# Splitting the input's first normalization into one batch a pass on GpSimd, and the bulk loads into pieces, in a four-layer attention kernel

## The reference

```
h = layernorm(x)                      # "LN0": no weight or bias, eps 1e-5
for l in range(4):
    xn = LN(h) * ln1_w + ln1_b
    q, k, v = xn@Wq.T+bq, xn@Wk.T+bk, xn@Wv.T+bv     # 16 heads of 8
    scores = (q.k + relshift((q+u).r)) / sqrt(8), causal
    h = h + softmax(scores) @ v @ Wo.T + bo
    h = h + gelu(LN(h) @ W1.T + b1) @ W2.T + b2      # inner size 512
x = x + h
x = x + moe(layernorm(x))             # 16 experts, top 4 in 2 of 4 groups, plus a shared one
```

## Time and profile before

| | |
|---|---|
| median of 3 runs | 2402.88 us |
| the profiled execution's own time | 2404.88 us |
| its span in the trace | 2403.1 us |
| PE busy | 2285.8 us (95%) |
| DVE busy | 2023.2 us (84%) |
| ACT busy | 1837.5 us (76%) |
| POOL busy | 1146.4 us (48%) |
| mean busy share of the DMA engines | 3 to 5 tenths until the expert part |

### The profile page before, as it was taken

The page is one execution under the profiler, slowest core; times in us unless marked ns, Lnnn a source line. Parts: engine busy times, 40 slices in busy tenths (PEclk is TensorE's granted clock), DMA queues, the critical chain, the costliest instruction groups (busy, mean ns, idle before and its releaser), DMA issues. The chain is left out here.

```text
span 2403.1 us, 83241 instructions
## 1 busy us (share of the span) xinstructions
PE 2285.8 (95%) x31360; PEld 1976.7 (82%) x31360; DVE 2023.2 (84%) x5071; ACT 1837.5 (76%) x2869; POOL 1146.4 (48%) x2089
## 2 busy tenths in 40 slices
PE   3899999999999999999999999999999999799998
PEld 3688888888888888888888888888888888677776
DVE  6789999888888888888888888888888886677774
ACT  2578888888888888888888888888878888655554
POOL 4355555554555555555454555555445553333332
PEclk8799999999999999999999999999999999899999
DMA  5543333333333333333333333333333331000000
GB/s 130 117 105 97 88 86 91 91 86 92 88 86 91 95 91 92 92 92 85 92 91 93 86 89 91 91 92 91 88 102 88 90 92 51 21 27 27 27 23 19
DMA packets 221161, 196.05 MB, mean 82 GB/s; under 512 B 28897, under 2 KB 217441, under 8 KB 220769
## 3 DMA queue, kind: packets, MB, share of 16 engines
q1 hardware_dynamic: 220768, 190.73, 29.8%
HBM read 14.46 MB, written 4.19 MB: 8 GB/s over the span
## 5 line engine op out<-in xcount | busy, mean ns | idle before, releaser
L1012 DVE TENSOR_REDUCE rowmax<-bank 128x4 f32<-128x1024 f32 (+1 forms) x768 | 914.2, 1218 | 103.3 <-PE bank L580 74.9
L817 ACT ACTIVATE probs<-bank 128x1024 f32<-128x1024 f32 x768 | 738.2, 1024 | 79.4 <-PE bank L640 78.8
L580 PE MATMUL bank<-kstack,qstack 62*128 62x256 f32 (+1 forms) x4096 | 417.9, 301 | 9.5 <-DMA qstack<-base 9.5
L640 PE MATMUL bank<-qstack,kstack 64*128 64x128 f32 (+1 forms) x4096 | 424.3, 300 | 0.0
L858 ACT ACT_TABLE_LOAD x256 | 328.4, 1283 | 4.5
L580 PEld LDWEIGHTS bank<-kstack,qstack 62*128 62x128 f32 x4096 | 317.4, 193 | 9.9 <-issue 9.9
L640 PEld LDWEIGHTS bank<-qstack,kstack 64*128 64x128 f32 x4096 | 317.1, 192 | 0.0
L602 PE MATMUL bank<-maskT_half,pick_half 64*128 64x128 bf16 (+1 forms) x3072 | 267.9, 241 | 24.5 <-DVE rowmax L1012 10.9
L542 PE MATMUL bank<-mask_half,pick_half 64*128 64x128 bf16 (+1 forms) x3072 | 268.8, 243 | 7.9 <-DVE h_all L1047 3.1
L725 PE MATMUL bank<-w,hidden 128*128 128x128 f32 x2048 | 272.6, 277 | 3.1 <-ACT hidden L867 3.1
L660 PE MATMUL bank<-probs,v_pad 128*32 128x256 f32 x4096 | 271.4, 382 | 0.6 <-DVE v_tok L993 0.6
(11 more groups left out here) (154 smaller groups left out, 5259.7 us busy)
## 6 DMA issues: line engine op xcount, KB each, us to landing
qstack<-base SPq DMA_DIRECT2D x768, 128.0 KB, 2.5
kstack<-base SPq DMA_DIRECT2D x384, 128.0 KB, 2.5
turn_x<-turn_c SPq DMA_DIRECT2D x512, 32.0 KB, 1.8
qstack<-maxrows SPq DMA_DIRECT2D x256, 16.0 KB
out<-ot SPq DMA_DIRECT2D x16, 256.0 KB, 2.4
xin<-in_x SPq DMA_DIRECT2D x14, 256.0 KB, 3.1
w<-in_w SPq DMA_DIRECT2D x4, 256.0 KB, 3.2
w_in<-in_w_in SPq DMA_DIRECT2D x1, 768.0 KB, 4.3
```

What stands on the lines that cost most here:

```text
L580: last = pe.matmul(bank[:, b0 + b, i * wide:(i + 1) * wide], qstack[rows, r, p0 + i, t * 128:(t + 1) * 128], kstack[rows, r, p0 + i, 0:wid ...
L640: last = pe.matmul(bank[:, b0 + b, i * wide:(i + 1) * wide], kstack[rows, r, p0 + i, kt * 128:(kt + 1) * 128], qstack[rows, r, p0 + i, q0: ...
L817: act.activation(probs[:, k], bank[:, A_BANK[k]:A_BANK[k] + 2, :], ACT.Exp, scale=SCALE).then_inc(exp_done[k], 1)
L1012: dve.tensor_reduce(rowmax[:, n % 2, t, :, p0:p0 + heads], bank[:, M_BANK[k]:M_BANK[k] + 2, :].rearrange("p b (h c) -> p b h c", h=heads), ...
```

## The change

LN0 groups become two of two batches (0 and 1, 2 and 3) and then 28 of one batch. From pass 1 to pass 28, each pass has `stats_0` of one batch (two tiles) on DVE, at the place where it stood, and `power_0` and a new `normalize_0` on POOL, at the place of `power_0`, ahead of the two `add_row`s. `apply_0` stays on DVE for groups 0 and 1 only; `stats_0(2)` and `power_0(2)` leave pass -1. The bulk loads are cut and spread: x in chunks of four batches (0.52 MB) in passes 1, 4, 7, 10, 13 and 16; b_o and w_o in pass 2; w_1 in pass 3; b_2 and b_1 in pass 4; w_2 by layer (0.26 MB) in passes 5, 7, 9 and 11; the q, k, v weights by layer (0.20 MB) in passes 12, 14 and 17. `split_w1(0)` moves on POOL from pass 3 to 4. Waits are divided accordingly (`middle_landed`, `later_landed`, `w_rest_landed`).

```diff
-PER = 2
-LN0_FIRST = 2
+LN0_STARTS = (0, 2) + tuple(range(4, 32))
+LN0_MOST = max(hi - lo for lo, hi in zip(LN0_STARTS, LN0_STARTS[1:] + (32,)))
-X_STARTS = (0, 2, 4, 8, 16, 24)
+X_STARTS = (0, 2, 4, 8, 12, 16, 20, 24, 28)
...
             def loads_behind(s):
-                if s == 1:
-                    rows_of_x(3)
                 if s == 2:
-                    sp.dma_start(b_o[:], on_all("bo")).then_inc(later_landed, 16)
+                    sp.dma_start(b_o[:], on_all("bo")).then_inc(middle_landed, 16)
+                    sp.dma_start(w_o[:], a["w_o"].rearrange("l p n -> p l n")).then_inc(middle_landed, 16)
+                if s == 3:
                     sp.dma_start(w_1[:], a["w_1"][0]).then_inc(w1_landed, 16)
-                    sp.dma_start(w_o[:], a["w_o"].rearrange("l p n -> p l n")).then_inc(later_landed, 16)
-                if s == 3:
+                if s == 4:
                     sp.dma_start(b_2[:], on_all("b2")).then_inc(later_landed, 16)
                     sp.dma_start(b_1[:], a["b_1"].rearrange("p (l c) -> p l c", l=LAYERS)).then_inc(later_landed, 16)
-                    sp.dma_start(w_2[:], a["w_2"].rearrange("l (c p) n -> p l c n", p=128)).then_inc(later_landed, 16)
-                if s in (4, 8):
-                    rows_of_x(3 + s // 4)
-                if s == 10:
-                    sp.dma_start(w_qkv[:, 1:LAYERS], a["w_qkv"].rearrange("l p n -> p l n")[:, 1:LAYERS]
-                                 ).then_inc(w_rest_landed, 16)
+                if s >= 5 and s % 2 == 1 and s // 2 - 2 < LAYERS:
+                    ly = s // 2 - 2
+                    sp.dma_start(w_2[:, ly], a["w_2"].rearrange("l (c p) n -> p l c n", p=128)[:, ly]
+                                 ).then_inc(later_landed if ly == 0 else w_rest_landed, 16)
+                if s >= 1 and s % 3 == 1 and 3 + s // 3 < len(X_STARTS):
+                    rows_of_x(3 + s // 3)
+                if s in (12, 14, 17):
+                    ly = 1 + (12, 14, 17).index(s)
+                    sp.dma_start(w_qkv[:, ly], a["w_qkv"][ly]).then_inc(w_rest_landed, 16)
...
             # DVE's pass
-                if s % PER == 0 and LN0_FIRST <= s // PER + 2 < B // PER:
-                    apply_0(s // PER + 2)
-                if s % PER == 1 and LN0_FIRST <= s // PER + 3 < B // PER:
-                    stats_0(s // PER + 3)
+                if 2 <= s + 1 < len(LN0_STARTS):
+                    stats_0(s + 1)
...
             # POOL
+            def normalize_0(g):
+                lo, hi = ln0_group(g)
+                pool.wait_ge(rstd0_ready, g + 1)
+                for i in range((hi - lo) * T):
+                    tile = h_all[:, lo + i // T, i % T]
+                    last = pool.tensor_scalar(tile, tile, mv0[:, i, 0:1], rstd0[:, i:i + 1], ALU.subtract, ALU.mult)
+                last.then_inc(ln0_done, 1)
...
-                if s > 0 and s % PER == 1 and LN0_FIRST <= s // PER + 3 < B // PER:
-                    power_0(s // PER + 3)
+                if 2 <= s + 1 < len(LN0_STARTS):
+                    power_0(s + 1)
+                    normalize_0(s + 1)
                 if live(s - 6):
-                    add_row(s - 6, b_2, xn2_ready, 2 * (s - 5), b2_added)
+                    add_row(s - 6, b_2, later_landed, LATER_DMAS, xn2_ready, 2 * (s - 5), b2_added)
                 if live(s - 4):
-                    add_row(s - 4, b_o, xn1_ready, 2 * (s - 3), bo_added)
+                    add_row(s - 4, b_o, middle_landed, MIDDLE_DMAS, xn1_ready, 2 * (s - 3), bo_added)
...
                 if s == -1:
                     power_0(1)
-                    power_0(2)
...
-                if s == 3:
+                if s == 4:
                     split_w1(0)
```

More of the change, by code:

```diff
@@ L99, in bank_left, with ln0_group @@
             return
+def ln0_group(g):
+    return (LN0_STARTS + (B,))[g:g + 2]
 def at_least(eng, sem, value):
@@ L239, in layers_program @@
         expo = sb("expo", [128, 16])
[L241 to L244, removed]
+        stats0 = sb("stats0", [128, LN0_MOST * T, 6])
+        mv0 = sb("mv0", [128, LN0_MOST * T, 2])
+        ve0 = sb("ve0", [128, LN0_MOST * T])
+        rstd0 = sb("rstd0", [128, LN0_MOST * T])
         stats1 = sb("stats1", [128, T, 6])
@@ L289, in layers_program @@
         consts_landed = sem("consts_landed")
+        middle_landed = sem("middle_landed")
         later_landed = sem("later_landed")
@@ L376, in layers_program @@
         CONST_DMAS = 4
-        LATER_DMAS = 5
+        MIDDLE_DMAS, LATER_DMAS, REST_DMAS = 2, 3, 2 * (LAYERS - 1)
         SLOTS = range(-LEAD, N + LAG)
@@ L691, in b3 @@
                 if n == 0:
-                    pe.wait_ge(later_landed, 16 * LATER_DMAS)
+                    pe.wait_ge(middle_landed, 16 * MIDDLE_DMAS)
                 bank_left(pe, (live(n + 3), max_done[4], n + 4), (live(n), ctxT_ready, n + 1))
@@ L722, in down @@
                     pe.wait_ge(gelu_done, FC * (n + 1))
+                    if n == 0:
+                        pe.wait_ge(later_landed, 16 * LATER_DMAS)
+                    if n == B:
+                        pe.wait_ge(w_rest_landed, 16 * REST_DMAS)
                     bank_left(pe, (live(n + 3), exp_done[5], n + 4), (live(n), gelu_done, FC * (n + 1)))
@@ L925, in stats_0 @@
             def stats_0(g):
-                dve.wait_ge(x_landed[sum(start <= g * PER for start in X_STARTS) - 1], 16)
+                lo, hi = ln0_group(g)
+                for c in range(len(X_STARTS)):
+                    if lo <= X_STARTS[c] < hi or X_STARTS[c] <= lo < (X_STARTS + (B,))[c + 1]:
+                        dve.wait_ge(x_landed[c], 16)
                 at_least(dve, rstd0_ready, g)
-                for i in range(PER * T):
-                    last = dve.bn_stats(stats0[:, i], h_all[:, g * PER + i // T, i % T])
+                for i in range((hi - lo) * T):
+                    last = dve.bn_stats(stats0[:, i], h_all[:, lo + i // T, i % T])
                 last.then_inc(stats0_done, 1)
                 dve.wait_ge(stats0_done, g + 1)
-                for i in range(PER * T):
+                for i in range((hi - lo) * T):
                     last = dve.bn_aggr(mv0[:, i], stats0[:, i])
@@ L936, in apply_0 @@
             def apply_0(g):
+                lo, hi = ln0_group(g)
                 dve.wait_ge(rstd0_ready, g + 1)
-                for i in range(PER * T):
-                    tile = h_all[:, g * PER + i // T, i % T]
+                for i in range((hi - lo) * T):
+                    tile = h_all[:, lo + i // T, i % T]
                     last = dve.tensor_scalar(tile, tile, mv0[:, i, 0:1], rstd0[:, i:i + 1], ALU.subtract, ALU.mult)
@@ L962, in stats_1 @@
             def stats_1(n):
-                dve.wait_ge(ln0_done, min(n, B - 1) // PER + 1)
+                dve.wait_ge(ln0_done, sum(start <= n for start in LN0_STARTS))
                 at_least(dve, h2_ready, n - B + 1)
@@ L1155, in power_0 @@
                 at_least(pool, ln0_done, g)
-                pool.tensor_scalar(ve0[:], mv0[:, :, 1], 1e-5, None, ALU.add).then_inc(ve0_ready, 1)
+                lo, hi = ln0_group(g)
+                c = (hi - lo) * T
+                pool.tensor_scalar(ve0[:, 0:c], mv0[:, 0:c, 1], 1e-5, None, ALU.add).then_inc(ve0_ready, 1)
                 pool.wait_ge(ve0_ready, g + 1)
-                pool.tensor_tensor(rstd0[:], ve0[:], expo[:, 0:PER * T], ALU.pow).then_inc(rstd0_ready, 1)
+                pool.tensor_tensor(rstd0[:, 0:c], ve0[:, 0:c], expo[:, 0:c], ALU.pow).then_inc(rstd0_ready, 1)
+            def normalize_0(g):
+                lo, hi = ln0_group(g)
+                pool.wait_ge(rstd0_ready, g + 1)
+                for i in range((hi - lo) * T):
+                    tile = h_all[:, lo + i // T, i % T]
+                    last = pool.tensor_scalar(tile, tile, mv0[:, i, 0:1], rstd0[:, i:i + 1], ALU.subtract, ALU.mult)
+                last.then_inc(ln0_done, 1)
             def power(ve, mv, rstd, mv_sem, ve_sem, rstd_sem, n):
@@ L1168, in split_qkv @@
                 at_least(pool, qk_done, B * (ly - 1))
-                if ly == 1:
-                    pool.wait_ge(w_rest_landed, 16)
+                if ly > 0:
+                    pool.wait_ge(w_rest_landed, 16 * REST_DMAS)
                 w, high = w_qkv[:, ly, 0:2 * D], w_now[:, ly % 2, 0]
@@ L1223, in v_padded, with add_row @@
                 last.then_inc(vpad_ready, 1)
-            def add_row(n, rows, read_sem, value, added_sem):
+            def add_row(n, rows, landed, dmas, read_sem, value, added_sem):
                 pool.wait_ge(read_sem, value)
                 if n == 0:
-                    pool.wait_ge(later_landed, 16 * LATER_DMAS)
+                    pool.wait_ge(landed, 16 * dmas)
                 h = h_all[:, n % B]
```

## The result

The changed kernel took 2444.07 us (median of 5, 2439.67 to 2446.11) against 2402.88 us before: a ratio of 1.0164, 95% interval 1.0151 to 1.0177, 41 us slower by the medians (39 by the ratio) where 7.8 us faster was forecast. Its profiled execution, 2439.67 us, is the fastest of the five, and that of before, 2404.88 us, is slower than its median, so the two spans differ by only 34.6 us.

A forecast was written before the change was run, and what follows sets the result against it. PE was taken to bound passes without LN0 or loads, DMA passes 0 to 5 and 8. Terms -9.0 (passes 0 to 5), -1.0 (steady loads) and +2.2 (LN0) gave -7.8: 2397.1 us profiled, 2395.1 median, range 2387 to 2402.

The forecast's parts named there:

- y: Time of two normalizations on POOL in each pass with LN0, taken as 0.62 us, 0.31 each.
- y - 0.02: Excess of each pass with LN0, 0.60 us in 23 passes: 13.8 us against 11.6 before, net +2.2.
- two of the large additions: Upper bound for POOL's two normalizations, 1.46 us, priced from two-input operations of 256 elements; it gives +21.5 us.
- a pass of LN0 over 16.3 us: Sign that the prediction is wrong, with POOL's two normalizations taking over 1 us.
- The slow rival: On POOL between power_0 and the add_rows: normalizations of 1.2 us set every pass, total 2408.4 us; chance 0.14.
- the rival in which the relief of DVE pays in full: DVE's load makes the LN0 passes' excess; a pass would cost 0.1 us, LN0 -9.3 us, total 2383.6; chance 0.08.
- the steady loads: Bulk loads in the steady passes after the fill: net -1.0 us, bounds -2.4 and +2.
- The fill: Passes 0 to 5, fewer bulk bytes ahead of the stacks: together -9.0 us, bounds -5 and -13.
- that term: Passes 4 and 5: fewer bytes in pass 4 shrink PE's wait for resid_1(0); -2.2 us, bounds 1.0 and 4.5.
- The rival of a fill that is paced by work: DVE and PE at low clock set passes 2 to 5; only -5.5 us comes back, total 2398.6; chance 0.18.
- a lone chunk of 0.52 MB: Chunks of x in passes 10, 13 and 16: set at no cost, with 0.3 us of margin as cover.
- part 1 and 2: Bulk bytes ahead of the stacks in passes 0 to 5, -9.0 us, and bulk in the steady passes, -1.0 us.

The follow-up runs named there:

- e3: The changed kernel with both add_rows on POOL moved ahead of power_0 and normalize_0; 2389.65 us, 0.9938 of the kernel before.
- e5: The changed kernel with POOL's order add_rows, normalize_0 of the group from the pass before, then power_0; 2387.14 us, 0.9926 of the kernel before.
- m1: A kernel of its own without the computation, timing POOL's elementwise forms and DVE's tensor_scalar beside POOL's additions; POOL's tensor_scalar with two SBUF scalars took 0.80 us.
- e6: The changed kernel with the bulk loads of before, so the LN0 part alone; 2449.53 us, 1.0185 of the kernel before.
- e2: The changed kernel with normalize_0 doing one tile of two, the other left out; 2406.14 us, 1.0017 of the kernel before.
- e9: The kernel before with both add_rows on POOL moved ahead of power_0; 2401.84 us, 0.9993 of the kernel before.
- e1: The kernel before with the cut and spread loads, their waits and split_w1(0) in pass 4, LN0 as before; 2395.74 us, 0.9969.
- e7: The changed kernel with normalize_0 moved on POOL behind the add_rows and the second power; 2390.55 us, 0.9948 of the kernel before.
- e8: e5 with loads_behind(s) issued on SP behind the stacks of unit s-1, ahead of maxima and exchange; 2376.00 us, 0.9884 of the kernel before.

## Why the prediction was wrong

**The step that failed is the size of y.** The prediction read the mechanism off rows 8 to 10: POOL waits for `stats_0`, and all that stands behind it up to the second power is on the path to `b2`; the change puts that in each pass. That is what happened in the changed kernel, and e3 and e5 show it by order alone. It priced the excess of a pass as y - 0.02 with y = 0.62, from a copy and a two-element `tensor_scalar`, "bounds y = 0.5 and 1.46". y was 1.59, outside both ends. I had taken the copy's slope on a small `tensor_scalar`, 0.31 us for one. m1 shows that this fails twice: with one operation and one immediate 128 elements take 0.53, and with two operations and two scalars from SBUF, which is what `normalize_0` is, 0.80, with a slope of 3.3 ns an element. The upper bound, "two of the large additions", was no bound for it. With the true y the formula gives 1.57 x 23 = 36.1 us, 24.5 more than the 11.6 of before: with the rest as forecast, 14.5 us slower. The sign that was named for this, a pass of LN0 over 16.3 us, came. The slow rival had the right place and mechanism, and a chance of 0.14; its price, y = 1.2, was too low as well.

**Two prices were missing.** POOL's later `add_row`s and `xn1_split` now run beside DVE's `maxparts` and `apply_2`, and the latter is 0.61 us longer. (`maxparts` is stretched too, but DVE still waits 1.11 us behind it, so that costs nothing.) The steps from an odd pass of before can be read one by one: `apply_2` starts 10.51 instead of 9.65 us after the copy, 0.86 later where the formula with the true y gives 0.82, and `b2` 1.47 later, 0.86 + 0.61. So 17.54 is 2.23 over 15.31, not 1.57, and the rest is (2.23 - 1.57) x 23 = 15.2 us; that it goes with the overlap, e3 and e5 show. And PE's gap ahead of `b2` grew to 1.76 us, and the clock falls in one pass of four: 5 x 1.46 = 7.3 us. That the gap is what lets it fall is argued, from this: in e6, which has the same gap of 1.76 us, it falls as often, in six passes, and in e2, with 0.81 us of gap, it does not fall from pass 6 to 28.

**The excess of before was read wrongly.** The prediction put 0.71 of an odd pass's 0.75 us down to POOL's chain, as `b2` was later by that much. But PE had already waited 0.54 us for DVE's row maxima ahead of `b2`, and e9, without the chain, gets back only 0.23. The number for the changed kernel did not hang on this, as it is counted from `stats_0` to `b2`. But the rival in which the relief of DVE pays in full (15.4 us a pass) was near what e5 reached, 15.33, once POOL's chain was out of the way too.

**The ledger** (the sum, profile against profile): passes 0 to 5, -5.2. Passes 6 to 28: 519.05 - 108.19 = 410.9 us against 479.84 - 113.37 = 366.5, +44.4; over 23 x 15.31 the new excess is 58.7 (36.1 + 15.2 + 7.3 = 58.6) and the old 14.3 (LN0 11.6, loads 2.7). So the steady loads gave 2.7 where 1.0 was forecast: at 17.54 us a pass, no copy waits for DMA any more. That makes +39.2 at pass 29. From there the profiled executions differ by 4.6 the other way, in pass 113 (1.4, where the profile of before has 3.4 us at a granted clock of 0.50 and the other none) and in the expert part, which the change does not touch. That this is chance between executions is not shown; the medians differ by 41.2.

**The fill:** -5.2 instead of -9.0, by its own terms. Pass 0 was 1.1 shorter (forecast 1.2), pass 1 1.5 (2.5), pass 2 1.3 (1.6). Pass 3 was 5.0 shorter, not 1.5. Two things changed there, the bytes and the clock. Pass 3 of the changed kernel, then of e1 and of e7, which have the same loads in the same place:

```profile
59.30:72.36 13.06, 9.03 (x114) 7.85 (x114) 10.38 (x23) 7.16 (x10) 6.90 (x13) 1.00 0.40 104
```

```profile
59.67:74.18 14.51, 11.06 (x112) 9.64 (x113) 10.69 (x27) 7.44 (x9) 6.33 (x12) 0.65 0.41 111
```

```profile
60.29:74.75 14.46, 10.84 (x112) 9.62 (x113) 9.84 (x22) 7.36 (x9) 6.88 (x13) 1.00 0.41 111
```

Before, the granted clock over this pass was 0.53 and the pass 18.01 us. With the cut loads it is 3.5 us shorter at a clock of 0.65 (e1) and as much shorter at 1.00 (e7); e3 and e5, at 0.63 and 0.64, have 4.0 and 3.9. So the fewer bytes gave most of it, at either clock, and DVE was no floor. Where the changed kernel has the last 1.0 to 1.5 us from stays open.

Then pass 4 came out 0.6 longer instead of shorter, and pass 5 3.2 longer: +3.8 where -2.2 was forecast. PE's wait for `resid_1(0)`, which was to shrink by 1.3 us, is 2.96 us and was 3.09, since PE arrived earlier and L851 of pass 5 still waited 6.57 us for the 0.79 MB ahead of its stacks. LN0's chain is part of pass 5 (PE idles 1.50 us ahead of `b2` there; with LN0 as before in e1, or out of the way in e3, the pass is 1.1 and 1.0 us longer than before), but it isn't what the fill lacks: pass 6 starts at 109.42 in e1 and at 108.17 in e3, no earlier than in the changed kernel. All three have passes 4 and 5 together 2.7 to 3.8 us longer than before, and e5 still 0.6, so that term had the wrong sign. Why pass 4 doesn't get shorter with fewer bytes ahead of its stacks stays open.

The rival of a fill that is paced by work named -5.5. That is near, but not by its reason: L851 of passes 1 to 5 is still released by DMA in the changed kernel, and with the loads out of the way (e8) pass 6 starts at 97.94. Only pass 3 fits its picture, and only in runs like e1, e3 and e5: there it ends with a copy that PE releases, at a low clock.

**The steady loads:** that a lone chunk of 0.52 MB costs a pass nothing holds, to 0.4 us, only for pairs of passes (e1).

**Right:** the direction of part 1 and 2 (e1: 7.5 us; of the 10.0 forecast, 8.8 were the loads' and 1.2 those of `stats_0(2)`, which e1 keeps); that relief of DVE brings nothing by itself while POOL's chain is longer; that both kinds of pass become alike. That this part came near is in part luck: by e1's profile the fill gave 4.0, not 7.8, and the steady passes 2.0, not 1.0; pass 3 gave more than forecast, passes 4 and 5 took it back, and the rest of the 7.5 lies behind the passes that the change touches.

## What to carry to other kernels

Before work moves to another engine, find the instruction that waits there and count what is queued behind it: here 54 us hung on whether two additions stood ahead of or behind that wait, and the added 1.6 us cost nothing where the engine was idle anyway. An operation that the trace doesn't show must be priced with an end well beyond its neighbours, or measured in a small kernel first. An instruction that starts late by some amount doesn't name the cause: look for an earlier wait on the same engine first, as with the 0.54 us here. For loads that share a queue with short transfers on the path, the place in the queue is worth about as much as the size.

## What the runs showed of the hardware

- GpSimd's `tensor_scalar` on one f32 tile of 128 elements takes 0.53 (one immediate) to 0.80 us (two scalars from SBUF), more than its two-input addition of the same size, 0.45.
- VectorE's `tensor_scalar` beside GpSimd's two-input additions took 0.70 us instead of 0.27 in one kernel; in another, one of them was held for 10.94 us, the whole of 16 additions in a row. Beside GpSimd's `tensor_scalar` it took 0.28, while GpSimd's took 0.94 instead of 0.78. A VectorE cast of 128x32 went from 0.17 to 0.69 us beside an addition.
- VectorE's two-input addition of 128 elements took 0.31 us instead of 0.21 beside GpSimd's copies.
- With a gap of 1.8 us in every 17.5 us pass, TensorE's clock was at the 1.2 GHz level for 3.4 us in one pass of four. Why in one of four was not tried.
